# A two-layer graph attention kernel: the order of TensorE's groups in layer 0, and the PSUM bank in which the row maximum is turned

## What is computed

```python
h = jnp.maximum(_layernorm(x, axis=-1), 0.0)
# layer 0
Whs = h @ Ws
Wht = h @ Wt
e = jnp.einsum('nh,mh->nm', Whs, Wht)
z = jnp.where(adj > 0, e, jnp.asarray(NEG, e.dtype))
alpha = jax.nn.softmax(z, axis=-1)
Whc = h @ Wc
h_prime = alpha @ Whc
...
x = x + h_prime
```

## Time and profile before

| | |
|---|---|
| median of three runs | 1365.22 us (1362.23 to 1365.72) |
| the profiled execution | 1368.26 us, of which the span is 1366.5 us |
| layer 0's sweep (first to last W) | 108.8 to 905.9 us of the span |
| busy share of PE, PEld, DVE, ACT | 93%, 83%, 76%, 72% |

### The profile page before, as it was taken

One profiled execution on the slowest core, in us unless ns is written; L12 is line 12 of the kernel. 1 busy time (PEld: TensorE's weight loads), 2 busy tenths in 40 slices (PEclk: granted clock), 3 DMA queues, 4 the chain that ended last, 5 costly groups with the idle time before them and its releaser, 6 DMA issues.

```text
span 1366.5 us, 75053 instructions
## 1 busy us (share of the span) xinstructions
PE 1273.9 (93%) x31691; PEld 1127.8 (83%) x31691; DVE 1044.2 (76%) x2196; ACT 984.7 (72%) x2100; POOL 165.8 (12%) x331
## 2 busy tenths in 40 slices
PE   4868899999999999999999999988999999899996
PEld 3657788888888888888888888876899999899996
DVE  6846467777776777677777767657999999989997
ACT  4855466666676666666666766676899998889995
POOL 4210111111111111111111111021000000000000
PEclk9979899999999999999999999999999999999999
DMA  9673799999999999999999999510334424324432
GB/s 188 77 94 62 93 129 134 140 141 126 141 138 137 128 139 142 128 136 141 139 126 138 141 133 134 103 41 4 99 90 119 123 84 127 111 80 125 113 95 74
DMA packets 103506, 157.58 MB, mean 115 GB/s; under 512 B 11456, under 2 KB 36288, under 8 KB 102848
## 3 DMA queue, kind: packets, MB, share of 16 engines
q0 software_dynamic: 36864, 67.13, 52.4%
q1 hardware_dynamic: 66496, 88.37, 20.2%
HBM read 314.84 MB, written 41.94 MB: 261 GB/s over the span
## 4 chain that ended last, share of the span: by engine, by line
PE 77%; issue 9%; ACT 8%; DVE 4%; DMA 1%; POOL 0%; ACTq 0%; SPq 0%; DVEq 0%; POOLq 0%
PE ps L884 17%; PE ps L787 16%; PE ps L734 11%; PE ps L858 9%; PE ps L766 6%; PE ps L749 4%; PE ps L761 4%; PE ps L722 4%; ACT arena L1118 3%; ACT arena L1127 3%; PE ps L775 1%; PE ps L663 1%; PE ps L881 1%; PE ps L665 1%; PE ps L639 1%
## 5 line engine op out<-in xcount | busy, mean ns | idle before, releaser
L787 PE MATMUL ps<-arena 128*128 128x129 f32 x2048 | 245.6, 278 | 0.0
L884 PE MATMUL ps<-arena 128*128 128x129 f32 x2048 | 244.5, 278 | 0.9 <-issue 0.9
L1134 ACT ACTIVATE arena<-ps,neg_max 128x1024 f32<-128x1024 f32 x128 | 142.3, 1112 | 133.5 <-PE ps L787 133.5
L884 PEld LDWEIGHTS ps<-arena 128*128 128x128 f32 x2048 | 236.1, 193 | 1.1 <-issue 1.1
L787 PEld LDWEIGHTS ps<-arena 128*128 128x128 f32 x2048 | 236.8, 193 | 0.0
L1487 DVE TENSOR_REDUCE mx<-ps 128x1 f32<-128x1024 f32 x128 | 156.8, 1225 | 99.2 <-PE ps L766 98.5
L1118 ACT ACTIVATE arena<-ps 128x512 f32<-128x512 f32 x256 | 152.7, 596 | 99.7 <-PE ps L734 99.7
L589 POOL DMA_DIRECT2D arena<-in_adjB x256 | 136.6, 534 | 687.3 <-PE ps L749 671.7
L1692 DVE TENSOR_SCALAR arena<-arena 128x128 f32<-128x128 f32 x768 | 203.3, 357 | 19.5 <-issue 11.3
L1112 ACT ACTIVATE arena<-ps 128x512 f16<-128x512 f32 x256 | 153.7, 600 | 42.5 <-PE ps L722 40.1
L734 PE MATMUL ps<-arena 128*32 128x128 f16 x8192 | 164.4, 222 | 17.4 <-issue 7.8
(11 more groups left out here) (164 smaller groups left out, 1320.1 us busy)
## 6 DMA issues: line engine op xcount, KB each, us to landing
arena<-in_adjB POOLq DMA_DIRECT2D x256, 256.0 KB, 8.0
sel_pick<-arena SPq DMA_DIRECT2D x64, 256.0 KB, 6.2
sel<-arena SPq DMA_DIRECT2D x64, 256.0 KB, 6.2
arena<-sel_pick SPq DMA_DIRECT2D x64, 256.0 KB, 3.8
arena<-sel SPq DMA_DIRECT2D x64, 256.0 KB, 2.8
arena<-in_xB SPq DMA_DIRECT2D x4, 1024.0 KB, 6.0
x_t<-in_x SPq DMA_DIRECT2D x64, 64.0 KB, 4.9
x_mid<-arena SPq DMA_DIRECT2D x64, 64.0 KB, 5.1
```

The source lines that it names most:

```text
L787: last = nc.tensor.matmul(pv_ps, p_T[:, s * P:(s + 1) * P], v_sel[:, b, s, :], start=False, stop=(s == SB - 1), skip_group_check=True)
L884: last = nc.tensor.matmul(xv_ps[b], w_msk[:, b, s, :], x1_sel[:, b, s, 0:VW], start=False, stop=(s == SB - 1), skip_group_check=True)
```

## The change

TensorE's groups are written in another order. A step is now:

S(c,3) M(a,1) V(c,2) K(a,1) W(d,0) T(c) V(c,3) M(a,2) K(a,2) W(d,1) M(a,3) V(a,0) W(d,2) P(e) W(d,3) K(a,3) S(a,0) S(a,1) V(a,1) M(e,0) K(e,0) S(a,2)

The second mask group of a tile moves from the end of one step to the start of the next, the W groups are spread over the step, and S(a,1) comes ahead of V(a,1). ACT's list of reads is changed to fit. T writes into columns 384 to 511 of bank 6, the bank of M, instead of bank 7, the bank of W. Its waits change with that: T waits until M(a,1) has been read (`m_evac`) and no longer for `y_ready`; M(a,2) waits for `top_done` of tile c; W(d,0) no longer waits for `top_done`.

```diff
--- before.py
+++ after.py
@@ -206,7 +206,7 @@
         pre_ps = ps[:, 6, 0:NB]
         early_ps = ps[:, 6, KV:KV + NB]
         pv_ps = ps[:, 7, 0:VW]
-        mx_ps = ps[:, 7, 256:256 + P]
+        mx_ps = ps[:, 6, 3 * P:4 * P]
         xg_ps = [ps[:, b, 0:3 * XW] for b in range(3)]
         xv_ps = [ps[:, 3 + b, 0:VW] for b in range(2)]
 
@@ -741,6 +741,8 @@
                 if q == 0:
                     pe.wait_ge(pick_ready, t + 1)
                 wait(pe, m_evac, t * 4 + q)
+                if q == 2:
+                    wait(pe, top_done, t)
                 settle()
                 mask = mask_8[t if isinstance(t, int) and t < 4 else b]
                 for s in range(4):
@@ -771,7 +773,7 @@
             def turn_maximum(t):
 
                 pe.wait_ge(mx_ready, t + 1)
-                wait(pe, y_ready, t - 1)
+                pe.wait_ge(m_evac, min(t * 4 + 6, TILES * 4) if isinstance(t, int) else t * 4 + 6)
                 nc.tensor.transpose(mx_ps, mx_b[:, :], ident[:, :]).then_inc(mx_turned, 1)
 
             def weigh(t, b, g):
@@ -780,7 +782,6 @@
                 pe.wait_ge(v_evac, t * 4 + (g + 1))
                 if g == 0:
                     wait(pe, y_ready, t)
-                    pe.wait_ge(top_done, min(t + 2, TILES) if isinstance(t, int) else t + 2)
                     nc.tensor.matmul(pv_ps, ones_b[:, :], mean_rows[0], start=True, stop=False, skip_group_check=True)
                 for k in range(4):
                     s = 4 * g + k
@@ -801,35 +802,39 @@
                     score_vectors(0, mg_ps)
                 if there(i, 3):
                     scores(c, cb, 3)
+                if there(i, 2):
+                    pick_mask(a, b, 1)
+                if there(i, 3):
                     pick_values(c, cb, 2)
                 if there(i, 2):
-                    pick_mask(a, b, 2)
                     pick_keys(a, b, 1)
+                if there(i, 4):
+                    weigh(d, b, 0)
                 if there(i, 3):
+                    turn_maximum(c)
                     pick_values(c, cb, 3)
                 if there(i, 2):
+                    pick_mask(a, b, 2)
+                    pick_keys(a, b, 2)
+                if there(i, 4):
+                    weigh(d, b, 1)
+                if there(i, 2):
                     pick_mask(a, b, 3)
-                if there(i, 3):
-                    turn_maximum(c)
-                if there(i, 2):
-                    pick_keys(a, b, 2)
                     pick_values(a, b, 0)
+                if there(i, 4):
+                    weigh(d, b, 2)
                 if within(i, EARLY + 1, TILES + 1):
                     prefix(e, pre_ps)
                 if there(i, 4):
-                    for g in range(4):
-                        weigh(d, b, g)
+                    weigh(d, b, 3)
                 if there(i, 2):
                     pick_keys(a, b, 3)
                     scores(a, b, 0)
+                    scores(a, b, 1)
                     pick_values(a, b, 1)
                 if there(i, 1):
                     pick_mask(e, cb, 0)
-                if there(i, 2):
-                    scores(a, b, 1)
-                if there(i, 1):
                     pick_keys(e, cb, 0)
-                    pick_mask(e, cb, 1)
                 if there(i, 2):
                     scores(a, b, 2)
 
@@ -1137,16 +1142,18 @@
 
             def tile_step(i, b):
                 e, a, c, cb = i - 1, i - 2, i - 3, 1 - b
+                if there(i, 2):
+                    take_mask(a, b, 1)
                 if there(i, 3):
                     take_values(c, cb, 2)
                 if there(i, 2):
-                    take_mask(a, b, 2)
                     take_keys(a, 1)
                 if there(i, 3):
                     take_values(c, cb, 3)
                 if there(i, 2):
+                    take_mask(a, b, 2)
+                    take_keys(a, 2)
                     take_mask(a, b, 3)
-                    take_keys(a, 2)
                 if there(i, 3):
                     exps(c, 0)
                 if there(i, 2):
@@ -1159,7 +1166,6 @@
                 if there(i, 1):
                     take_mask(e, cb, 0)
                     take_keys(e, 0)
-                    take_mask(e, cb, 1)
 
             first_preparation()
             tile_sweep(act, tile_step)
```

## The result

The changed kernel takes 1404.81 us (median, 1401.86 to 1405.99) against 1365.47 us for the kernel before in its runs on the same chip: a ratio of 1.028, 95% interval 1.027 to 1.030. It is 39 us slower. The forecast was 57 us slower, 1422 us, with a range of 1400 to 1448.

The account below looks back on a forecast made before the run. TensorE, nearly always busy, was taken as the bound before; afterwards a DVE-TensorE loop. Its terms 3.12 + 0.14 + 3.5 + 0.24 + 4.10 + 2.38 = 13.48 us against 12.53, times 60 steps, add 57 us: 1422 us, range 1400 to 1448.

Parts of the forecast that it names:

- Z: The second L1487 of a step on DVE (L1493 after the change), where the forecast's round starts and ends.
- 5 DVE, `place` to L1493: DVE's list from `place` to the step's first L1487 (now L1493), put at 4.10 us, between 4.02 and 4.3.
- 6 DVE, L1493 to Z: DVE from the step's first L1487 (now L1493) to Z, put at 2.38 us, between 2.35 and 2.4.
- The ring: Loop from Z through DVE's maximum, TensorE's M(a,2) to P(e), and DVE's list back to Z: 13.48 us a step.
- lower bounds: Smallest values of the loop's terms on DVE and TensorE, together 13.17 us a step, giving 1402 us.
- item 3: TensorE from M(a,2) to P(e), six groups, put at 3.5 us, between 3.44 and 4.04.
- Does the ring decide: Whether DVE reaches Z later than S(a,3) allows: 10.22 against 9.34 us after M(a,2), so 0.88 us late.
- TensorE's idle: TensorE waiting about 1.4 us a step, partly at T(c) and partly at M(a,2).
- Rival 1: TensorE's idle gaps close and nothing replaces them: 12.09 us a step, 26 us less, 1339 us; chance 0.05.
- Rival 2: DVE isn't late, so the loop closes over S(a,3): 12.6 us a step, about 1369 us; chance 0.07.
- Rival 3: Mask loads land up to 1.3 us too late for DVE's L1459: 78 us more, 1500 us; chance 0.04.
- Rival 4: TensorE's clock falls to 1.2 GHz from M(a,2) to P(e): 210 us more, 1632 us; chance 0.03.

Follow-up runs that it names:

- e3_no_turn: Changed kernel without T: DVE reduces the spread maximum untransposed, and M(a,2) waits for nothing of DVE; 1323.56 us, ratio 0.968.
- e8_keys_ahead: Changed kernel with maximum(c) ahead of indicate(e, 1), and K(a,3), then P(e), ahead of W(d,2); 1339.26 us, ratio 0.981.
- e2_prefix_early: Changed kernel with P(e) ahead of W(d,2) instead of behind it; 1391.26 us, ratio 1.017.
- e5_before_max_first: Kernel before the change, with DVE's maximum(c) moved ahead of indicate(e, 1); 1470.25 us, ratio 1.077.
- e7_extra_ring: Changed kernel with one additional, useless DVE reduction of 1024 elements a step, ahead of denominator(d); 1500.0 us, ratio 1.099.
- e9_weigh_behind: Changed kernel with W(d,1) and W(d,2) moved to stand with W(d,3) behind P(e); 1406.33 us, ratio 1.030.
- e1_max_first: Changed kernel with DVE's maximum(c) moved ahead of indicate(e, 1); 1362.14 us, ratio 0.997.
- e10_bank_alone: Kernel before the change, in its own order, with T turned in bank 6 instead of bank 7; 1430.44 us, ratio 1.048.

## Why the prediction was right, point by point

The mechanism is shown: DVE comes late to Z, TensorE waits at T and M(a,2), DVE's spare time is one block ahead of `place`. Of the sum, 0.95 us a step was forecast and 0.69 measured, over 57 steps' worth instead of 60. The items, from the timeline above:

| item | forecast | measured |
|---|---|---|
| 1 DVE, Z to the end of the maximum | 3.12 | 3.11 |
| 2 DVE's end to M(a,2) | 0.14 | 0.10 |
| 3 TensorE, M(a,2) to P(e) | 3.5 | 3.61 |
| 4 P(e) to `place` | 0.24 | 0.23 |
| 5 DVE, `place` to L1493 | 4.10 | 3.94 |
| 6 DVE, L1493 to Z | 2.38 | 2.25 |
| sum | 13.48 | 13.24 |

- **The ring's length.** The mis-sized terms are 5 and 6. L1516 to L1523 is 0.41 where 0.32 was taken, and the rest is equal or shorter. Where nothing is waited for, the next DVE instruction starts 0.10 us after L1488 (0.22 taken) and 0.20 after L1526 (0.33 taken), and L1493 starts 1.12 us after L1465 (1.24 taken). In the earlier trace rows the places ahead of L1510, L1487 and Z were waits, and I had put a gap where the instructions in fact overlap. The lower bounds of both items, 4.02 and 2.35, were already too high. So that the ring still came out at 13.24, 0.07 us above the sum of all lower bounds, and the time at 1404.81, 3 us above the lower one, is in part luck: item 3 was longer than taken, and made up for some of it.
- **TensorE's part.** W(d,1) takes 1.07 and W(d,2) 1.00 where 0.905 was taken, so single fp32 groups do cost 0.1 to 0.16 more, 0.26 together; M followed by V takes 0.23 instead of 0.33 and gives 0.10 of it back. e3_no_turn says that over a step the two cancel.
- **Does the ring decide.** 0.88 us late was forecast; it is 1.74 - 0.87 = 0.87.
- **TensorE's idle.** 1.4 us was forecast, 1.1 to 1.2 measured: 11.7 / 30 ahead of T and 25.0 / 31 ahead of M(a,2).
- **Rival 1** (12.09 us, 1339 us) is what e8_keys_ahead reaches, with 12.17 us and 1339.26 us. It was a fair price for the order, which the change didn't get. By the Trainium skill's rule (Perfetto Trace Analysis, Identifying the Most-Contended Engine) TensorE was the engine to work on; the trace agrees that it leads, busy 94.01 of 100 us in the changed kernel. The waits that the edit opened, 1.15 us a step, are set by DVE, which is busy 65.35.
- **Rival 2** (the loop through S(a,3)) decides in e2_prefix_early, at 12.86 us instead of 12.6, as P(e) then waits for a read.
- **Rival 3** (late loads): the median load lands after 7.9 us, and DVE waits for them 0.7 us in the whole sweep.
- **Rival 4** (the clock): 1.00 in the changed kernel. It falls at times in e5_before_max_first, e7_extra_ring and e9_weigh_behind.

## What to carry to other kernels

When a reorder fills the gaps of the busiest engine, follow each result that another engine needs soon (here P) to its new place, and sum the loop that it closes, from one instruction back to the same one a step later: an engine that is busy 72% of the time (65% after the change) can decide the step if its idle time has been gathered where it has nothing to do. Moving a wait is a change for everything behind it on that engine; what helps in one order (e1_max_first, 43 us less than the changed kernel) can cost in another (e5_before_max_first, 104 us more than the kernel before). A group put between two others to cover a read only pays if it isn't also ahead of what the ring waits for; a shorter one from outside the ring did both here.

## What the runs showed of the hardware

The clock in e7_extra_ring. Its longest waits of TensorE, from 300 to 700 us, are 1.6 us ahead of T and 0.8 us ahead of M(a,2), with V between. Over 500 to 600 us the granted clock was 0.96, and within it whole stretches lie lower (columns as above):

```profile
495.00:500.00 5.00, 2.96 (x73) 2.41 (x72) 3.18 (x7) 1.70 (x4) 0.53 (x1) 0.88 0.99 109
500.00:505.00 5.00, 5.00 (x89) 4.50 (x89) 1.18 (x2) 2.19 (x4) 0.53 (x1) 0.78 0.88 74
505.00:510.00 5.00, 5.00 (x166) 4.23 (x164) 4.60 (x8) 3.79 (x7) 0.96 (x2) 1.00 0.82 144
```

In the second of these a V group (501.37) took 1.00 us instead of 0.62: the lower level, 1.2 GHz. So 0.55 us of the mean step of 14.94 are clock. In this kernel every stretch at the lower level from 200 to 880 us lies between a maximum and the next P(e), that is on item 3 of the ring, where a slow group is late for DVE in full: such steps take 15.9 us among steps of 14.4.

The changed kernel, with at most 0.5 and 0.8 us of idle at the same two places, stays at 1.00, and so does e10_bank_alone with 1.0 us ahead of T in each step. e5_before_max_first, with 1.25 us ahead of P(e) in each, is at 0.98:

```profile
500.00:600.00 100.00, 88.70 (x2305) 77.45 (x2298) 63.83 (x98) 59.46 (x100) 14.77 (x28) 0.98 0.94 120
```

A single wait of 2.6 us in e2_prefix_early (ahead of M(a,2) at 494.11) brought no fall, and e9_weigh_behind, with three waits of 0.3 to 0.4 us in each step, had four from 200 to 880 us (0.93 from 380 to 430). So what sets off a fall is not settled by the length of a wait alone, and these runs leave it open. The Trainium skill, TensorE: Matmul & The Clock Gate, section A second HAM failure mode: psum-queue depth-cycling, describes a clock that swings with short idles between groups of matmuls; here the trace agrees in e7_extra_ring (0.96) and e5_before_max_first (0.98), and not in the changed kernel (1.00).
